# Deformable sampling: ScalarE forms distances and hats of four steps at a time, in place of two

## The chip, the cores and the metric

The kernel runs on one core of one Trainium2 chip. The metric is the device time of one execution in microseconds. Three runs of the kernel before stand for it; their median is 12080.69 us.

## What is computed

The reference is a chain of four layers on x of 2x192x96x96 (f32), each of which normalises x in groups, applies its block and adds the result to x. The change concerns the first, a pair of deformable 3x3 convolutions on 180 channels:

```python
xr = conv1x1(x, w_reduce, b_reduce)
offs = conv1x1(xr, w_offset, b_offset)
off_w, off_h = (offs[:, :cm], offs[:, cm:])
f_w = deform_conv2d(xr, off_w, w_dcnw, b_dcnw)
f_h = deform_conv2d(xr, off_h, w_dcnh, b_dcnh)
f_avg = (f_w + f_h).mean(axis=(2, 3), keepdims=True)
attn = jax.nn.softmax(conv1x1(f_avg, w_attn, b_attn), axis=1)
f_dcm = attn[:, 0:1] * f_h + attn[:, 1:2] * f_w
return conv1x1(f_dcm, w_expand, b_expand)
```

Each output pixel reads, for each of 10 channel groups and 9 taps, xr at a place given by an offset, interpolated between four pixels. The other layers (an edge filter with a 1x1 convolution, a recurrent mixing in two directions, a selective scan) aren't touched.

## The kernel before

`program` runs nine phases one after another; only `sample_and_convolve` is changed. It treats the image as 144 tiles of 128 pixels (72 in each of two images), 12 tiles to a turn of the loop. A tile has 20 steps: two convolutions times ten channel groups. Two neighbouring steps are a pair and share one slot of the buffer HX, which has RP = 8 slots. A tile reads five, five or six candidate rows in turn (`ROWSOF`); the number sets how wide the sampling matmuls are (90 or 108 columns).

Sampling along x is a matmul with interpolation weights, max(0, 1-|x-p|), as the matrix. Five engines work on it, each with an order of its own, written out by hand and held together by semaphores:

- SyncE, `pair_load` (L790 to L794): waits for a free slot (s_free, L791), then loads the sampling places of one pair, broadcast to 96 partitions, 2304 elements in each (864 KB), and raises the slot's own semaphore s_bx. Eight slots are free at the start. Every third tile the input rows are loaded too (`chunk_load`, L766, 675 KB), behind the first pair of that tile; row data, sums and stores of a tile are issued between pairs.
- ScalarE, `distance` (L828 to L831): waits for the slot's s_bx and writes |place - p| in place; `hats` (L833 to L837): waits for one distance to be done (s_ab, L835) and writes max(0, 1-d) in place, and raises s_hx by 2, one for each step. `row_weights` (L839 to L850) does four small instructions in each tile for the weights along y (Abs at L847, Relu at L850; the waits for VectorE are L843 and L845). Its loop runs AHEAD = 12 steps ahead by index: at step n it issues the distance of pair (n+12)/2+1 and then the hats of pair (n+12)/2. The small ones come at steps 4, 5, 9 and 10 of a tile.
- TensorE: at step n (two at a time) it transposes what VectorE summed (L912), then calls `sample` for steps n+6 and n+7. Each first waits for s_pt (L918) and then for s_hx (L879), and makes 18 matmuls (36 records) at L884. Then it convolves (L925). The first of these matmuls gives back one slot (s_free).
- VectorE multiplies the samples with the weights along y (`weigh`, L1019) and, with GpSimd (`halve`, L955), sums over rows; s_pt comes out of this.

```python
                    for n in range(NBB):
                        i, j = n // NB, n % NB
                        if n % 2 == 0:
                            distance((n + AHEAD) // 2 + 1)
                            hats((n + AHEAD) // 2)
                        if j in (4, 5, 9, 10):
                            row_weights((i + 1) % NRB, (4, 5, 9, 10).index(j))
```

Of the kernel before, what the change touches and what calls it, by code (L numbers as in the profile page):

```python
# [9 lines left out]
ACT = mybir.ActivationFunctionType  # L10
# [687 lines left out]
def sample_and_convolve(nc, k):  # L698
# [10 lines left out]
    NRB = 12  # L709
    NBB = NB * NRB  # L710
    NPX = TAPS * 128
    RP, AHEAD, LEAD = 8, 12, 6
    EXTRA = AHEAD // 2 + 1
    LEN = TAPS * CG
    NPR = NG // 2
    pieces = [range(2 * LEN * g // 128, 2 * LEN * (g + 1) // 128) for g in range(NPR - 1)]
# [1 line left out]
    with Phase(nc, "dc") as p:  # L718
# [4 lines left out]
        HX = p.sb([W, RP, 2, NPX])  # L723
# [9 lines left out]
        QX = p.sb([W, 1])  # L733
# [8 lines left out]
        s_bx = p.sems(RP)  # L742
# [6 lines left out]
        def loops(e, body):  # L749
            nw = e.value_load(k.FLAG[0:1, 0:1], min_val=1, max_val=NWIN)  # L750
            for b in range(B):
                for y2 in range(NT // NRB):
                    with e.Fori(0, nw) as w:
                        body(b, y2, w)

        with p.block() as blk:
            @blk.sync
            def _(e):
# [10 lines left out]
                def row_loads(i, b, ti, y):  # L769
                    for h in range(2):  # L770
                        at = 384 * (y // 3) + 64 * TILES[y % 3][h]
                        e.dma_start(OYT[64 * h:64 * h + 64, i % 2, :], k.oyd_v[b][at:at + 64]).then_inc(s_row[i % 2], 16)
                    e.dma_start(TAB[:, i % 2, :],
                                k.d["c_tab"][DS(ti, 1)].rearrange("a p c -> (a p) c")).then_inc(s_row[i % 2], 16)
# [5 lines left out]
                def store_tile(i, at, sem):  # L780

                    e.wait_ge(s_out, 2).then_inc(s_out, -2)
                    dst = k.d["fd"][DS(at, 1)].rearrange("y c (h p) x -> p (c h) (y x)", p=HM)
                    e.dma_start(dst, FT[:, i % 2, :, :]).then_inc(sem, 16)
# [5 lines left out]
                def pair_load(slot, b, y, q):  # L790
                    e.wait_ge(s_free, 1).then_inc(s_free, -1)  # L791
                    src = k.d["sxd"][b, DS(y, 1)].rearrange("a c (q k) x -> (a c q) (k x)", q=5)
                    src = src[q:q + 1, :].partition_broadcast(W)
                    e.dma_start(HX[:, slot, :, :].rearrange("p u n -> p (u n)"), src).then_inc(s_bx[slot], 16)  # L794
# [17 lines left out]
                row_loads(0, 0, 0, 0)  # L812
                for q in range(EXTRA):
                    pair_load(q, 0, 0, q)
                    if q == 0:
                        chunk_load(0, 0, 0)
                e.wait_ge(s_sb, 16).then_inc(s_sb, -16)
                e.wait_ge(s_free, RP + 2 - EXTRA).then_inc(s_free, EXTRA - 2 - RP)
                store_tile(0, B * NT, s_fin)
# [3 lines left out]
            @blk.scalar  # L823
            def _(e):
                e.dma_start(WD[:, :, :, :], k.d["w_dcn"]).then_inc(s_w, 16)
                e.wait_ge(s_qx, 16).then_inc(s_qx, -16)

                def distance(q):  # L828

                    e.wait_ge(s_bx[q % RP], 16).then_inc(s_bx[q % RP], -16)  # L830
                    e.activation(HX[:, q % RP, :, :], HX[:, q % RP, :, :], ACT.Abs, bias=QX[:, 0:1]).then_inc(s_ab, 1)  # L831

                def hats(q):  # L833

                    e.wait_ge(s_ab, 1).then_inc(s_ab, -1)  # L835
                    e.activation(HX[:, q % RP, :, :], HX[:, q % RP, :, :], ACT.Relu, bias=1.0, scale=-1.0)\  # L836
                        .then_inc(s_hx, 2)  # L837

                def row_weights(i, step):  # L839

                    o = slice(step // 2 * HM * ROWSOF[i % 3], (step // 2 + 1) * HM * ROWSOF[i % 3])
                    if step % 2 == 0:
                        e.wait_ge(s_rw, 2).then_inc(s_rw, -2)  # L843
                    if step == 0:
                        e.wait_ge(s_hyf, 1).then_inc(s_hyf, -1)  # L845
                    if step % 2 == 0:
                        e.activation(V[:, o], V[:, o], ACT.Abs).then_inc(s_va2, 1)  # L847
                    else:
                        e.wait_ge(s_va2, 1).then_inc(s_va2, -1)
                        e.activation(HY[:, i % 2, o], V[:, o], ACT.Relu, bias=1.0, scale=-1.0).then_inc(s_hy, 1)  # L850

                for step in range(4):
                    row_weights(0, step)
                distance(0)
                for q in range(AHEAD // 2):
                    distance(q + 1)
                    hats(q)

                def body(b, y2, w):
                    for n in range(NBB):  # L860
                        i, j = n // NB, n % NB
                        if n % 2 == 0:
                            distance((n + AHEAD) // 2 + 1)
                            hats((n + AHEAD) // 2)
                        if j in (4, 5, 9, 10):
                            row_weights((i + 1) % NRB, (4, 5, 9, 10).index(j))

                loops(e, body)
                e.wait_ge(s_ab, 1).then_inc(s_ab, -1)
                e.wait_ge(s_hyf, 1).then_inc(s_hyf, -1)  # L870
# [1440 lines left out]
def mamba_scan(nc, k):  # L2311
# [8 lines left out]
    with Phase(nc, "ms") as p:  # L2320
# [256 lines left out]
        with p.block() as blk:  # L2577
# [12 lines left out]


PHASES = (first_norm_and_projections, far_samples, sample_and_convolve, mix_and_expand, edges_and_merge,
          wkv, gate_and_project, mamba_inputs, mamba_scan)

# [121 lines left out]
```

## Time and profile before

| | |
|---|---|
| median of three runs | 12080.69 us (12080.34 to 12087.21) |
| the profiled execution's own time | 12053.83 us |
| its span | 12051.9 us |
| mean granted clock of TensorE | 0.955 |
| busy: TensorE / ScalarE / VectorE / GpSimd | 11074.3 / 10353.3 / 9815.6 / 5059.6 us |
| the sampling stage | about 620 to 7220 us |

Busy time is the union of an engine's instructions. Matmuls are pipelined and their ends are modelled, so a matmul row's length holds a small overlap with the next row; starts are the better measure. "Idle before" is the time an engine stood still ahead of an instruction, with what ended it. A name such as "PEq L879" is a semaphore wait of that line on the engine's own queue. Where several waits stand at one place, the trace names one of them, and it may have been another that held.

### The profile page before, as it was taken

The numbers are of one execution on the slowest core, as the hardware profiler recorded it, in microseconds if no ns is written. First come the engines' busy times: TensorE is split into PE (matmuls) and PEld (weight loads), VectorE is DVE, ScalarE is ACT, GpSimd is POOL, SyncE is SP. The second block draws the span as 40 slices with busy tenths as digits, with TensorE's granted clock in tenths as the row PEclk, the third lists the DMA queues.
The fourth block names the chain that finished last, engine by engine and source line by source line (L and its number), as shares of the span: only waits on it lengthen the run. The fifth ranks groups of instructions, "written<-read, shape, count | busy, mean of one in ns | idle before, by whom it ended". The sixth has DMA issues, their size and how long they took to land. (4 is left out here: it accounts for less than half of the span.)

```text
span 12051.9 us, 337397 instructions
## 1 busy us (share of the span) xinstructions
PE 11074.3 (92%) x133078; PEld 8457.9 (70%) x133078; DVE 9815.6 (81%) x14111; ACT 10353.3 (86%) x10426; POOL 5059.6 (42%) x3633
## 2 busy tenths in 40 slices
PE   6689999999999999999999999850899899999999
PEld 4389999999999999999999984420633455555555
DVE  4578888888888888888888886799878788888888
ACT  3299999999999999999999993596778899998998
POOL 0033333333333433343333430133200588888887
PEclk9899999999999999999999995985999899999999
DMA  6488888888888888888888888444544333333332
GB/s 165 129 223 213 214 218 217 218 214 211 215 214 214 217 216 219 218 219 216 215 216 215 219 205 198 136 163 132 171 150 156 116 101 102 108 101 103 101 101 85
DMA packets 818421, 2128.02 MB, mean 177 GB/s; under 512 B 145699, under 2 KB 414369, under 8 KB 674497
## 3 DMA queue, kind: packets, MB, share of 16 engines
q1 hardware_dynamic: 800912, 2072.13, 64.3%
q10 hardware_dynamic: 15120, 30.71, 0.7%
q8 instruction: 1080, 17.69, 0.7%
q14 instruction: 477, 3.90, 0.1%
q0 software_dynamic: 832, 3.59, 0.1%
HBM read 1782.85 MB, written 323.30 MB: 175 GB/s over the span
## 5 line engine op out<-in xcount | busy, mean ns | idle before, releaser
L884 PE MATMUL dc_p<-dc_t 96*64 96x90 f32 (+1 forms) x103896 | 4658.9, 247 | 144.9 <-issue 71.7
L884 PEld LDWEIGHTS dc_p<-dc_t 96*64 96x64 f32 x103896 | 4370.8, 136 | 418.1 <-issue 416.4
L955 POOL TENSOR_TENSOR dc_t<-dc_t 128x324 f32<-128x324 f32 (+1 forms) x2885 | 2591.8, 898 | 4028.3 <-DVEq L1043 2738.2
L1019 DVE TENSOR_TENSOR dc_t<-dc_p,dc_t 128x810 f32<-128x810 f32 (+1 forms) x2886 | 3043.5, 1055 | 896.4 <-DVEq L1016 861.1
L831 ACT ACTIVATE dc_t<-dc_t 96x2304 f32<-96x2304 f32 x1447 | 3189.0, 2204 | 105.6 <-ACTq L830 104.5
L836 ACT ACTIVATE dc_t<-dc_t 96x2304 f32<-96x2304 f32 x1446 | 3049.9, 2109 | 0.0
L2545 DVE TENSOR_TENSOR_SCAN ms_t<-ms_t,ms_p 128x512 f32<-128x512 f32 x1728 | 2127.0, 1270 | 283.7 <-PE ms_p L2487 203.7
L2461 POOL TENSOR_TENSOR ms_t<-ms_t 128x1536 f32<-128x1536 f32 x576 | 1987.9, 3456 | 503.3 <-DVE ms_t L2545 499.6
L2497 PE MATMUL ms_p<-ms_t,top_t 128*128 128x512 f32 x3456 | 1774.7, 596 | 0.0
L925 PE MATMUL dc_p<-dc_t 128*128 128x180 f32 (+1 forms) x7488 | 1536.5, 337 | 3.4 <-issue 2.0
L2487 PEld LDWEIGHTS ms_p<-top_t,ms_t 128*128 128x128 f32 x6912 | 850.9, 141 | 966.4 <-issue 693.8
L925 PEld LDWEIGHTS dc_p<-dc_t 128*128 128x128 f32 (+1 forms) x7488 | 1137.7, 190 | 177.7 <-issue 9.2
L2433 ACT ACTIVATE ms_t<-ms_t 128x384 f32<-128x384 f32 x2304 | 1222.2, 602 | 24.2 <-PE ms_p L2487 24.1
L2440 ACT ACTIVATE ms_t<-ms_t 128x512 f32<-128x512 f32 x1728 | 1114.1, 708 | 0.0
L2487 PE MATMUL ms_p<-top_t,ms_t 128*128 128x128 f32 x6912 | 1049.3, 275 | 56.4 <-DVE ms_t L2545 50.5
L1045 DVE TENSOR_TENSOR dc_t<-dc_t 128x324 f32<-128x324 f32 x1442 | 730.8, 507 | 0.0
L1005 DVE COPY dc_t<-dc_p 128x256 f32<-128x256 f32 (+1 forms) x1440 | 673.8, 468 | 11.7 <-DVEq L1000 7.5
L912 PE MATMUL dc_p<-top_t,dc_t 128*128 128x128 f32 (+1 forms) x3744 | 646.9, 273 | 0.6 <-issue 0.3
L979 DVE TENSOR_TENSOR dc_t<-dc_t 128x225 f32<-128x225 f32 (+1 forms) x580 | 410.2, 708 | 250.6 <-DVEq L977 250.4
L2497 PEld LDWEIGHTS ms_p<-ms_t,top_t 128*128 128x128 f32 x3456 | 522.2, 191 | 15.7 <-DVE ms_t L2555 11.4
L912 PEld LDWEIGHTS dc_p<-top_t,dc_t 128*128 128x128 f32 (+1 forms) x3744 | 496.2, 140 | 18.9 <-issue 1.4
L1034 DVE TENSOR_TENSOR dc_t<-dc_t 128x324 f32<-128x324 f32 x962 | 465.2, 484 | 0.4 <-issue 0.2
(258 smaller groups left out, 9527.7 us busy)
## 6 DMA issues: line engine op xcount, KB each, us to landing
dc_t<-sxd SPq DMA_DIRECT2D x1447, 864.0 KB, 6.1
ms_t<-bcd SPq DMA_DIRECT2D x576, 256.0 KB, 3.3
dc_t<-xrT SPq DMA_DIRECT2D x49, 675.0 KB, 9.7
kvd<-wk_t SPq DMA_DIRECT2D x18, 1536.0 KB, 5.1
szd<-mi_t SPq DMA_DIRECT2D x36, 768.0 KB, 4.4
xvd<-mi_t SPq DMA_DIRECT2D x36, 768.0 KB, 4.8
dld<-mi_t SPq DMA_DIRECT2D x36, 768.0 KB, 3.4
ms_t<-dld SPq DMA_DIRECT2D x36, 768.0 KB, 6.8
```

The lines of the kernel that those rows point to most:

```text
L831: e.activation(HX[:, q % RP, :, :], HX[:, q % RP, :, :], ACT.Abs, bias=QX[:, 0:1]).then_inc(s_ab, 1)
L836: e.activation(HX[:, q % RP, :, :], HX[:, q % RP, :, :], ACT.Relu, bias=1.0, scale=-1.0)\
L884: ins = e.matmul(PT[j % 2][o:o + 64, t // 3, t % 3 * nr * CG:(t % 3 + 1) * nr * CG], HX[:, m // 2 % RP, m % 2, t * 128 + o:t * 128 + o + 6 ...
L912: ins = e.transpose(PR[0:o, u * 128:(u + 1) * 128], VA[:, n // NG % 2, 128 * c:128 * c + o], k.ident[:, :])
L925: ins = e.matmul(PF[:, conv * CM:(conv + 1) * CM], VT[0:o, n // 2 % 2, u, :], WD[0:o, c, conv, :], start=(c == 0), stop=(c == NCK - 1), sk ...
L955: e.tensor_tensor(ZH[:, n % 4, :, 0:m], z[:, :, 0:m], z[:, :, nr * CG - m:nr * CG], ALU.add)\
L1019: e.tensor_tensor(Zt[:, n % 4, 0:nr * LEN].rearrange("p (b m i) -> p b m i", b=3, i=CG), PT[n % 2][:, :, 0:3 * nr * CG].rearrange("p b (m ...
L2433: ins = e.activation(BU[:, i % RT, tb, :], UT[:, c % 2, tb, 0:DI], ACT.Copy, scale=UT[:, c % 2, tb, DI + n:DI + n + 1])
L2461: e.tensor_tensor(G[:, i % RG, :, :], HH[:, i % RH, :, :], CB[:, i % RB, :].unsqueeze(1).to_broadcast([128, ND, T]), ALU.mult).then_inc(s_ ...
L2487: ins = e.transpose(PB[:, d, tb * 128:(tb + 1) * 128], BU[:, i % RT, tb, d * 128:(d + 1) * 128], k.ident[:, :])
L2497: e.matmul(PY[:, d, :], k.ident[:, :], G[:, i % RG, d, :], start=(n == 0), stop=(n == NS - 1))\
L2545: e.tensor_tensor_scan(HH[:, i % RH, d, :], DA[:, i % RA, d, :], PB[:, d, :], CAR[:, n, d:d + 1], ALU.mult, ALU.add).then_inc(s_scan, 1)
```

## The change

ScalarE treats two slots, four steps, in one instruction. `distance` waits for the loads of both slots and `hats` raises s_hx by 4. The loop goes over every fourth step: at step n it issues the distance of quad (n+12)/4+1 and the hats of quad (n+12)/4. The small instructions of a tile come at its steps 4 and 8: the first of two between distance and hats, the second behind the hats. EXTRA, the number of loads issued behind the loop so that ScalarE's lead is served, is 8 in place of 7. The number of slots, the loads, TensorE's order and where it gives slots back, VectorE and GpSimd are as before.

```diff
-    EXTRA = AHEAD // 2 + 1
+    EXTRA = AHEAD // 2 + 2
...
-                def distance(q):
-
-                    e.wait_ge(s_bx[q % RP], 16).then_inc(s_bx[q % RP], -16)
-                    e.activation(HX[:, q % RP, :, :], HX[:, q % RP, :, :], ACT.Abs, bias=QX[:, 0:1]).then_inc(s_ab, 1)
-
-                def hats(q):
-
+                def distance(r):
+
+                    o = 2 * r % RP
+                    e.wait_ge(s_bx[o], 16).then_inc(s_bx[o], -16)
+                    e.wait_ge(s_bx[o + 1], 16).then_inc(s_bx[o + 1], -16)
+                    e.activation(HX[:, o:o + 2, :, :], HX[:, o:o + 2, :, :], ACT.Abs, bias=QX[:, 0:1]).then_inc(s_ab, 1)
+
+                def hats(r):
+
+                    o = 2 * r % RP
                     e.wait_ge(s_ab, 1).then_inc(s_ab, -1)
-                    e.activation(HX[:, q % RP, :, :], HX[:, q % RP, :, :], ACT.Relu, bias=1.0, scale=-1.0)\
-                        .then_inc(s_hx, 2)
+                    e.activation(HX[:, o:o + 2, :, :], HX[:, o:o + 2, :, :], ACT.Relu, bias=1.0, scale=-1.0)\
+                        .then_inc(s_hx, 4)
...
-                for q in range(AHEAD // 2):
-                    distance(q + 1)
-                    hats(q)
+                for r in range(AHEAD // 4):
+                    distance(r + 1)
+                    hats(r)
...
-                    for n in range(NBB):
+                    for n in range(0, NBB, 4):
                         i, j = n // NB, n % NB
-                        if n % 2 == 0:
-                            distance((n + AHEAD) // 2 + 1)
-                            hats((n + AHEAD) // 2)
-                        if j in (4, 5, 9, 10):
-                            row_weights((i + 1) % NRB, (4, 5, 9, 10).index(j))
+                        distance((n + AHEAD) // 4 + 1)
+                        if j in (4, 8):
+                            row_weights((i + 1) % NRB, j // 2 - 2)
+                        hats((n + AHEAD) // 4)
+                        if j in (4, 8):
+                            row_weights((i + 1) % NRB, j // 2 - 1)
```

Lines below move down by up to 5: distance is L833, hats L839, row weights L850 and L853 in the changed kernel.

ScalarE's order at the start of the loop, first before and then changed. dc_s49 to dc_s56 are s_bx of the eight slots (a slot's load has landed), dc_s22 is s_ab (a distance is done), dc_s34, dc_s35 and dc_s37 are the row weights' own; L831 and L833 are distances, L836 and L839 hats, the 128x450 rows are row weights:

```order
L831 ACTIVATE dc_t<-dc_t 96x2304 [waits dc_s56]
L836 ACTIVATE dc_t<-dc_t 96x2304 [waits dc_s22]
L831 ACTIVATE dc_t<-dc_t 96x2304 [waits dc_s49]
L836 ACTIVATE dc_t<-dc_t 96x2304 [waits dc_s22]
L831 ACTIVATE dc_t<-dc_t 96x2304 [waits dc_s50]
L836 ACTIVATE dc_t<-dc_t 96x2304 [waits dc_s22]
L847 ACTIVATE dc_t<-dc_t 128x450 [waits dc_s34,dc_s35]
L850 ACTIVATE dc_t<-dc_t 128x450 [waits dc_s37]
```

```order
L833 ACTIVATE dc_t<-dc_t 96x4608 [waits dc_s49,dc_s50]
L839 ACTIVATE dc_t<-dc_t 96x4608 [waits dc_s22]
L833 ACTIVATE dc_t<-dc_t 96x4608 [waits dc_s51,dc_s52]
L850 ACTIVATE dc_t<-dc_t 128x450 [waits dc_s34,dc_s35]
L839 ACTIVATE dc_t<-dc_t 96x4608 [waits dc_s22]
L853 ACTIVATE dc_t<-dc_t 128x450 [waits dc_s37]
L833 ACTIVATE dc_t<-dc_t 96x4608 [waits dc_s53,dc_s54]
L850 ACTIVATE dc_t<-dc_t 128x450 [waits dc_s34]
L839 ACTIVATE dc_t<-dc_t 96x4608 [waits dc_s22]
L853 ACTIVATE dc_t<-dc_t 128x450 [waits dc_s37]
```

Before, each distance waits for one load, and the hats behind it are those of the slot before. Now each distance waits for two, so the hats of four steps have two more loads ahead of them, and two small instructions stand one on each side of the hats.

ScalarE's order ahead of the loop, where the first hats are made, before and then changed:

```order
L831 ACTIVATE dc_t<-dc_t 96x2304 [waits dc_s49]
L831 ACTIVATE dc_t<-dc_t 96x2304 [waits dc_s50]
L836 ACTIVATE dc_t<-dc_t 96x2304 [waits dc_s22]
L831 ACTIVATE dc_t<-dc_t 96x2304 [waits dc_s51]
L836 ACTIVATE dc_t<-dc_t 96x2304 [waits dc_s22]
```

```order
L833 ACTIVATE dc_t<-dc_t 96x4608 [waits dc_s49,dc_s50]
L833 ACTIVATE dc_t<-dc_t 96x4608 [waits dc_s51,dc_s52]
L839 ACTIVATE dc_t<-dc_t 96x4608 [waits dc_s22]
L833 ACTIVATE dc_t<-dc_t 96x4608 [waits dc_s53,dc_s54]
L839 ACTIVATE dc_t<-dc_t 96x4608 [waits dc_s22]
```

The first hats stood behind two loads and two distances of 2304 elements; now they stand behind four loads and two distances of 4608.

## Rows read from the trace of the kernel before

**Rows 1.** Windows: length; busy PE, PEld, DVE, ACT, POOL; granted clock, DMA share, GB/s.

```profile
620.00:7220.00 6600.00, 6474.70 (x115705) 6009.12 (x115706) 5427.51 (x9082) 6293.03 (x3469) 2591.75 (x2885) 0.99 0.85 216
...
4053.00:4058.00 5.00, 4.60 (x42) 4.32 (x42) 2.72 (x4) 4.84 (x3) 1.06 (x2) 0.66 0.40 92
```

**Rows 2.** Costliest groups: xcount | busy us, mean ns | idle before, releaser.

```profile
L831 ACT ACTIVATE dc_t<-dc_t 96x2304 f32<-96x2304 f32 x1447 | 3189.0, 2204 | 105.6 <-ACTq L830 104.5
L836 ACT ACTIVATE dc_t<-dc_t 96x2304 f32<-96x2304 f32 x1446 | 3049.9, 2109 | 0.0
```

**Rows 3.** Waits, 700 to 7300 us: waiter <- ended by: us, times, longest.

```profile
ACT dc_t L847 <- ACTq L845: 177.2, 126, 3.3
...
PE dc_p L884 <- issue: 68.1, 81, 2.5
...
PE dc_p L884 <- PEq L879: 31.6, 49, 2.8
```

**Rows 4.** Waits of SyncE's queue, 3000 to 5000 us.

```profile
SPq L791 <- SPq L791: 1645.2, 439, 8.9
```

**Rows 5.** Timeline of TensorE: start us, length us, line, count.

```profile
4021.03 3.55 PE L884 MATMUL dc_p<-dc_t 96*64 96x108 f32 x72
...
4045.03 3.55 PE L884 MATMUL dc_p<-dc_t 96*64 96x108 f32 x72
...
4053.40 2.61 PE L884 MATMUL dc_p<-dc_t 96*64 96x108 f32 x34 [1.70 <-issue]
...
4072.68 3.01 PE L884 MATMUL dc_p<-dc_t 96*64 96x90 f32 x72
...
4081.14 3.01 PE L884 MATMUL dc_p<-dc_t 96*64 96x90 f32 x72
4084.08 1.18 PE L925 MATMUL dc_p<-dc_t 128*128 128x180 f32 x6
...
4093.98 3.01 PE L884 MATMUL dc_p<-dc_t 96*64 96x90 f32 x72
...
4098.06 3.01 PE L884 MATMUL dc_p<-dc_t 96*64 96x90 f32 x72
...
4138.34 3.01 PE L884 MATMUL dc_p<-dc_t 96*64 96x90 f32 x72 [0.94 <-PEq L879]
...
4197.99 3.55 PE L884 MATMUL dc_p<-dc_t 96*64 96x108 f32 x72
```

**Rows 6.** Pair loads L794: one near 4084.7, one near 4182.8, then all 439 of 3000 to 5000.

```profile
L794 SPq DMA_DIRECT2D dc_t<-sxd x1: 303/303/303, 4084.7 to 4084.7; - x1
...
DMA to landing us min/median/max: 6.1/6.1/6.1
...
L794 SPq DMA_DIRECT2D dc_t<-sxd x1: 310/310/310, 4182.8 to 4182.8; - x1
...
DMA to landing us min/median/max: 8.9/8.9/8.9
...
DMA to landing us min/median/max: 5.2/6.1/10.5
```

**Rows 7.** Timeline of ScalarE.

```profile
4084.30 2.11 ACT L836 ACTIVATE dc_t<-dc_t 96x2304 f32<-96x2304 f32 x1
4086.31 2.20 ACT L831 ACTIVATE dc_t<-dc_t 96x2304 f32<-96x2304 f32 x1
4088.42 2.11 ACT L836 ACTIVATE dc_t<-dc_t 96x2304 f32<-96x2304 f32 x1
4090.97 2.22 ACT L831 ACTIVATE dc_t<-dc_t 96x2304 f32<-96x2304 f32 x1 [0.45 <-ACTq L830]
...
4125.51 2.11 ACT L836 ACTIVATE dc_t<-dc_t 96x2304 f32<-96x2304 f32 x1
```

**Rows 8.** ScalarE's groups by shape, 800 to 7100 us.

```profile
L850 ACT ACTIVATE dc_t<-dc_t 128x450 f32<-128x450 f32 x185 | 105.8, 572 | 10.9
...
L850 ACT ACTIVATE dc_t<-dc_t 128x540 f32<-128x540 f32 x92 | 59.5, 647 | 5.4
```

## The prediction

> **What bounds the kernel now.** First I read the windows of the trace to find the stage: the change lies wholly between 620 and 7220 us. There the matmul rows of TensorE cover 6474.7 of 6600 us, ScalarE's 6293.0, VectorE's 5427.5, and the DMA engines are busy 0.85 of the time [rows 1]. TensorE sets the pace; all that could ever be won on it here is the 125 us in which it is idle. Then the groups: distance and hats (2204 and 2109 ns each, 2304 elements) make up almost all of ScalarE's time, and before the distances it stood idle for loads for 104.5 us in all [rows 2]. Third, the waits: TensorE's own at the sampling line are few (68.1 and 31.6 us), and ScalarE's longest is the one ahead of the row weights (177.2 us, L845) [rows 3]. The 31.6 us carry the name L879, which is the wait for hats. But one of them ends at 4138.34 [rows 5], and the hats of that pair were written by 4125.51+2.11 = 4127.62 [rows 7]: they had been ready for 10.7 us, so another wait of the same place held TensorE, the one for VectorE's and GpSimd's work on the sums (s_pt). SyncE waits before every load it issues [rows 4]: L791 is the wait for a free slot (439 waits for 439 loads), so a load starts as soon as TensorE gives one back. So three engines run round a ring: slot freed, load, distance, hats, sampling, slot freed. What matters is how much slack this ring has, not how busy ScalarE is.
>
> I number the pairs of steps (a slot holds one pair) 0, 1, 2, ... through the stage. When the pair p has been sampled, TensorE's next matmul at L925 frees the slot for load p+7. An example: sampling ends and L925 starts at 4084.08 [rows 5]; the load is issued at 4084.7 and lands 6.1 us later [rows 6]; the distance of that pair starts at 4090.97, at once [rows 7]. The pair two before it in the slots has its hats at 4084.30 to 4086.41 [rows 7] and wasn't sampled until 4098.06 [rows 5]: pair 756, ready 11.7 us early. That float of 10 to 12 us is why TensorE doesn't wait for ScalarE today.
>
> **The change, part by part.** *ScalarE's own work.* Now a distance is followed by its neighbour 2.11 us later and hats by theirs 2.01 us later (4086.31, 4088.42 and the rows around) [rows 7]. The element rate comes from the row weights: 90 elements more take 647-572 = 75 ns, 0.83 ns each [rows 8], so 2304 more elements add 1.92 us. For four steps: 4.03+3.93 = 7.96 us instead of 2x4.12 = 8.24. That is 0.28 us saved in each of 720 quads, 202 us of ScalarE's time. None of it is on the path, since TensorE doesn't wait for ScalarE: the cover is the float, which the next part spends.
>
> *What the quad waits for.* Before, the hats of pair p needed load p+1 (the distance of p+1 is issued ahead of them). Now the hats of pairs p, p+1 (p even) need load p+3, because the distance ahead of them covers p+2 and p+3. Nothing is loaded earlier: there are still eight slots, freed one by one at the same matmul, and SyncE issues the same loads in the same order, save one more at the end. So the wait ends two pairs later, 8.5 to 9.6 us, and both instructions behind it run 1.92 us longer before anything of them counts, together 12.4 to 13.4 us later. Against the float the ring closes or falls short.
>
> *The ring, counted directly.* From the issue of load p+3 to the start of sampling pair p TensorE walks four pairs less one sampling, and less the 0.66 us between L925 and the issue. In a tile with five candidate rows five pairs take 4093.98-4072.68 = 21.30 us, 4.26 each, and a sampling 2.94 (its 3.01 less the overlap); in one with six rows 4045.03-4021.03 = 24.00, 4.80 each, and 3.48 [rows 5]. So there are 4x4.26-0.66-2.94 = 13.4 us, or 4x4.80-0.66-3.48 = 15.1 us. The chain wants landing 6.1 (the median of 439 [rows 6]), 0.11 to the distance, 4.03 for it and 4.03 for the hats: 14.3 us.
> - Five rows: short by 0.8 us. In the example: hats would end at 4090.97+8.06 = 4099.03, sampling was due at 4098.06, short by 0.97.
> - Six rows: 0.8 us to spare.
> - In two quads of five (loop index j 4 and 8) a row-weights instruction now stands between distance and hats. It takes 572 or 647 ns [rows 8], and less the overlap of some 0.1 us that neighbours on ScalarE show (hats 2.11 long, the next start 2.01 later [rows 7]) I take 0.5.
> - Every third tile SyncE loads the 675 KB of input rows behind the tile's first pair, and the next pair, an odd one, which is the kind a quad waits for, lands late: 8.9 us in the example. From 4182.8 to 4197.99, when pair 778 was sampled, are 15.2 us [rows 6, 5]; wanted are 8.9+0.11+8.06+0.5 = 17.6: short by 2.4.
>
> *The sum.* Three tiles hold 15 quads. Ten of them have five rows: 10x0.83 + 4x0.5 = 10.3 us short. But the window of each quad also holds TensorE's wait at the quad before, so a steady shortness is paid once in two quads: 5.2 us. Plus 2.4 for the late load: 7.6 us per three tiles, 48 times in 144 tiles, 365 us. From this I take off two things. A wait before an even pair leaves a gap ahead of the odd load, which then lands sooner; landings range down to 5.2 us [rows 6], and I take 0.2 us of relief, near the median since the DMA engines stay busy: 10x0.2/2x48 = 48. And some of the new waits fall where TensorE is idle anyway; of the 125 us [rows 1] I take a quarter, 30. I add 12 us once at the start, where the first hats now need four loads rather than two (864 KB at 216 GB/s, 4.1 us each [rows 1]) and both instructions are 1.92 us longer. VectorE and GpSimd do the same as before and wait as they do now; their slack grows, cost 0. The waits of ScalarE ahead of the row weights [rows 3] will mostly go, since the weights now come after a later load; nothing is gained by it. Net: 365-48-30+12 = +299 us. Against the profiled execution's 12053.8 that is 12353; the median of the runs shown, 12080.7, is 27 us above it, so I forecast 12380.
>
> The ends. Were every critical load to land at 5.2, the shortness of five-row quads goes and the late load costs 1.5: 48x1.5+12 = 84 us, 12165. Were no wait shared between quads, 48x(10.3+2.4) = 610 us, 12690; since the window argument excludes most of that, I go a good half of the way.
>
> **The rivals.**
> *A. The clock falls at the new waits.* After a wait of 1.70 us (the row at 4053.40) 34 matmuls took 2.61 us, where 72 take 3.55 otherwise, and the granted clock of the 5 us window there is 0.66 [rows 5, 1]. Part of those 5 us ran at the lower level, 1.2 GHz; 5x(1-0.66) = 1.7 us of work were lost. For it: the waits behind the late loads are 2.4 us. Against: the common ones are under 1 us, and the wait of 0.94 us before 4138.34 was followed by a normal 3.01 [rows 5]. At 48 such places: 82 us more, 12460. Chance 0.2.
> *B. Faster: the saved overhead counts.* In five-row tiles ScalarE's ten pairs (41.2) and four weights (about 2) fill more than TensorE's 42.6 us. If TensorE's present waits come from ScalarE's lateness, the 202 us remove them. This decides if landings shrink below about 5.3 us, so that the ring closes in all tiles. Price: the half of 125 us, 12020. Against: hats stood ready 10.7 and 11.7 us ahead, in one case at the very wait that carries the hats' line as its name. Chance 0.07. The Trainium skill, Advanced Engine Details and Errata, section TRN2 Errata, holds that a bubble stands between ScalarE instructions and advises large tiles to make it small: by that rule this change is a gain. The rows agree that it saves ScalarE 0.28 us a quad; they don't show that this time is on the path.
> *C. No difference: the ring gives way.* With TensorE slower, traffic falls: in the 5 us window after that stall the DMA share was 0.40 [rows 1]. If landings drop near 5.2 and late ones hide in existing waits, only the start's 12 us are left: 12093. Against: the late load is slow because 1539 KB are in flight, and a short wait doesn't change that. Chance 0.08. The Trainium skill, DMA: Bandwidth & Descriptors, section Latency and other measured facts, has the fixed part of a transfer shrink when HBM is less loaded, which speaks for C; the spread of landings agrees in direction, and no row here gives the size at an idle HBM.
>
> **How the numbers follow.** Forecast 0.65, A 0.20, B 0.07, C 0.08. A measurement of this kernel can tell about 0.2%, 24 us, from no change. So slower 0.85, same 0.08, faster 0.07. The range takes in the forecast's own low end, A, and half of the way to the high end: 12165 to 12560; it leaves out B and C.
>
> **What would show it.** In the changed profile: distance and hats near 4120 and 4030 ns, 720-odd each; the stage about 300 us longer, with TensorE waiting at the sampling line in the first sampling of a quad, 0.5 to 1 us in five-row tiles, longest (2 to 3 us) once in three tiles; ScalarE waiting for loads at the distance (hundreds of us, not 104), and hardly ahead of the row weights; DMA share under 0.85. Wrong if TensorE's idle time in the stage stays at 125 us (C) or falls (B); if granted clock falls well under 0.99, A.

## The result and the profile after

The changed kernel takes 12520.52 us in the median of four runs (12499.26 to 12524.19), the kernel before on the same chip 12083.95 us. The ratio is 1.0354, with a 95% interval of 1.0336 to 1.0372: slower by 3.5%, 437 us. The forecast was 12380 in a range of 12165 to 12560, so the sign and the range hold, and the loss forecast, 299 us, is two thirds of the one measured.

The page of the changed kernel, busy time by engine and the groups that answer to [rows 2] (xcount | busy, mean ns | idle before, releaser):

```profile
span 12497.3 us, 335231 instructions
...
PE 11186.5 (90%) x133078; PEld 8553.3 (68%) x133078; DVE 9834.1 (79%) x14111; ACT 10170.4 (81%) x8980; POOL 5009.1 (40%) x3633
...
L888 PE MATMUL dc_p<-dc_t 96*64 96x90 f32 (+1 forms) x103896 | 4740.3, 250 | 481.1 <-PEq L883 379.5
...
L833 ACT ACTIVATE dc_t<-dc_t 96x4608 f32<-96x4608 f32 x724 | 2994.6, 4136 | 937.8 <-ACTq L832 935.9
L839 ACT ACTIVATE dc_t<-dc_t 96x4608 f32<-96x4608 f32 x723 | 2913.6, 4030 | 0.0
```

ScalarE did what was intended: 183 us less busy time (10170.4; 10353.3 before). It now stands idle for 936 us ahead of the distances, waiting for loads (104.5 before). TensorE's idle time ahead of the sampling matmuls went from 144.9 us (the page before, L884) to 481.1, and its busy time for the same 133078 matmuls from 11074.3 to 11186.5. These two, 336 and 112 us, come to 448 us; the span grew by 445. Taken from the trace, the stage from its first sampling to its last takes 7019 us, 6586 before: 433 of the 445 us lie in it.

The waits from 700 to 7700 us, as in [rows 3]; L883 is the wait for hats, L832 the wait for the quad's second load:

```profile
ACT dc_t L833 <- ACTq L832: 918.7, 543, 7.1
...
PE dc_p L888 <- PEq L883: 333.4, 314, 5.2
...
PE dc_p L888 <- issue: 95.8, 91, 2.7
```

The 49 waits under the hats' line have become 314, and now the name is right: 315 quads behind the first find TensorE waiting at their start, and in 312 of them sampling starts within 0.2 us of the hats' end. The ring, followed once round at pair 736: the last load that its hats need, that of pair 739, is issued at 4193.0 and lands 6.0 us later; then ScalarE, then TensorE's sampling:

```profile
L794 SPq DMA_DIRECT2D dc_t<-sxd x1: 303/303/303, 4193.0 to 4193.0; - x1
...
DMA to landing us min/median/max: 6.0/6.0/6.0
```

```profile
4199.13 4.14 ACT L833 ACTIVATE dc_t<-dc_t 96x4608 f32<-96x4608 f32 x1 [6.18 <-ACTq L832]
4203.18 4.03 ACT L839 ACTIVATE dc_t<-dc_t 96x4608 f32<-96x4608 f32 x1
```

The sampling row is cut off by the end of the window that was asked for:

```profile
4207.35 0.88 PE L888 MATMUL dc_p<-dc_t 96*64 96x90 f32 x17 [0.96 <-PEq L883]
```

The distance starts 0.1 us behind the landing, the hats 4.05 us later, they end at 4207.21, and sampling starts 0.14 us after. Nothing in this chain waits for anything but its forerunner. TensorE waited 0.96 us for it, in the place and of the size that the forecast named for a five-row tile.

And the late load behind the input rows. TensorE waits 2.33 us for it in the mean of its 48 times. The longest of these waits, behind a load that landed 11.7 us after its issue (9.65 in the mean of the 48), in the timeline of TensorE, with the windows around it (length; busy PE, PEld, DVE, ACT, POOL; granted clock, DMA share, GB/s):

```profile
4107.40 3.55 PE L888 MATMUL dc_p<-dc_t 96*64 96x108 f32 x72
...
4117.52 6.63 PE L888 MATMUL dc_p<-dc_t 96*64 96x108 f32 x72 [5.24 <-PEq L883]
```

```profile
620.00:7640.00 7020.00, 6572.71 (x115539) 6093.57 (x115540) 5437.03 (x9067) 6091.94 (x2019) 2538.07 (x2880) 0.98 0.79 202
...
4117.00:4124.00 7.00, 6.48 (x72) 6.44 (x72) 1.57 (x2) 7.00 (x5) 1.06 (x1) 0.51 0.06 18
```

After a wait of 5.24 us the 72 matmuls of a six-row pair took 6.63 us instead of 3.55; the granted clock of that window is 0.51, the lower level, 1.2 GHz. That is 3.1 us on top of the wait. Counted over the whole stage, 55 pairs have sampling matmuls that take over 0.33 us each (0.24 to 0.26 otherwise), 18 before; 31 of the 55 stand right behind the wait for the late load.

### The profile page after: what moved, and what is told of

It is laid out like the page before. It is cut to its first block and busy times, and to the rows that moved or that the text cites. A ratio compares the mean times of both kernels' runs of the same rounds, so it can differ in the third digit from the quotient of the medians.

```text
span 12497.3 us, 335231 instructions
## 1 busy us (share of the span) xinstructions
PE 11186.5 (90%) x133078; PEld 8553.3 (68%) x133078; DVE 9834.1 (79%) x14111; ACT 10170.4 (81%) x8980; POOL 5009.1 (40%) x3633
## 5 line engine op out<-in xcount | busy, mean ns | idle before, releaser
L888 PE MATMUL dc_p<-dc_t 96*64 96x90 f32 (+1 forms) x103896 | 4740.3, 250 | 481.1 <-PEq L883 379.5
L888 PEld LDWEIGHTS dc_p<-dc_t 96*64 96x64 f32 x103896 | 4455.7, 138 | 770.1 <-issue 767.3
L959 POOL TENSOR_TENSOR dc_t<-dc_t 128x324 f32<-128x324 f32 (+1 forms) x2885 | 2541.9, 881 | 4518.6 <-DVEq L1047 2920.9
L833 ACT ACTIVATE dc_t<-dc_t 96x4608 f32<-96x4608 f32 x724 | 2994.6, 4136 | 937.8 <-ACTq L832 935.9
L839 ACT ACTIVATE dc_t<-dc_t 96x4608 f32<-96x4608 f32 x723 | 2913.6, 4030 | 0.0
```

What stands on the lines that cost most here:

```text
L833: e.activation(HX[:, o:o + 2, :, :], HX[:, o:o + 2, :, :], ACT.Abs, bias=QX[:, 0:1]).then_inc(s_ab, 1)
L839: e.activation(HX[:, o:o + 2, :, :], HX[:, o:o + 2, :, :], ACT.Relu, bias=1.0, scale=-1.0)\
L888: ins = e.matmul(PT[j % 2][o:o + 64, t // 3, t % 3 * nr * CG:(t % 3 + 1) * nr * CG], HX[:, m // 2 % RP, m % 2, t * 128 + o:t * 128 + o + 6 ...
L959: e.tensor_tensor(ZH[:, n % 4, :, 0:m], z[:, :, 0:m], z[:, :, nr * CG - m:nr * CG], ALU.add)\
```

## The experiments

The theory: the loss is the ring's lateness, counted from the landing of load p+3 to the sampling of pair p, plus the clock that falls after the longest waits. The rivals: the long instructions cost by themselves; waiting for two loads at once costs, whatever comes behind; ScalarE's order doesn't matter; the kernel before was held by ScalarE's fullness. Each kernel ran in turn with the kernel before on the same chip; ratios are to that. Two experiments are compared by their ratios too, since the kernel before has medians from 12067 to 12084 us in the three sets of runs.

**e1: short instructions, long waits.** The changed kernel's order and waits, with instructions of one slot:

```diff
-                    e.activation(HX[:, o:o + 2, :, :], HX[:, o:o + 2, :, :], ACT.Abs, bias=QX[:, 0:1]).then_inc(s_ab, 1)
+                    for u in range(2):
+                        e.activation(HX[:, o + u, :, :], HX[:, o + u, :, :], ACT.Abs, bias=QX[:, 0:1]).then_inc(s_ab, 1)
...
+                    for u in range(2):
+                        e.wait_ge(s_ab, 1).then_inc(s_ab, -1)
+                        e.activation(HX[:, o + u, :, :], HX[:, o + u, :, :], ACT.Relu, bias=1.0, scale=-1.0)\
+                            .then_inc(s_hx, 2)
```

> Instructions of 2304 elements again, but in the changed kernel's order and with its waits (two loads, distance, distance, hats, hats). Ring theory (loss = how late the first hats of a quad end against TensorE's four-pair window): the first hats end 2.11+2.11+2.11 = 6.3 us after the loads instead of 8.06, 1.75 us sooner. Five-row quads then have about 0.8 us to spare, only the late load behind the input rows is still short, by 1 us at most: 12130 to 12200 us, TensorE idle in the stage about 170 us. Rival (waiting for two loads at once costs, whatever the instructions' length): stays near 12520. Rival (the long instructions themselves cost): back to 12084.

Measured: 12175.78 us, ratio 1.0077 (1.0059 to 1.0094). The two loads are waited for just as in the changed kernel, but four fifths of the loss are gone. Handing over the first half of a quad 1.75 us sooner is enough for most quads. So waiting for two loads at once is not what costs, whatever comes behind. The first rival, that the long instructions cost by themselves, asked for the whole loss to go, and 0.8% stays; this run alone doesn't settle it, e2 does. TensorE's idle time ahead of sampling shows the remnant:

```profile
L890 PE MATMUL dc_p<-dc_t 96*64 96x90 f32 (+1 forms) x103896 | 4675.8, 247 | 242.1 <-PEq L885 125.6
```

**e2: long instructions, short wait.** Hats directly behind their own distance, so that they need load p+1:

```diff
-                        distance((n + AHEAD) // 4 + 1)
+                        distance((n + AHEAD) // 4)
```

(and the same ahead of the loop, with 6 loads behind it instead of 8).

> Instructions of 4608 elements, but the hats of a quad come directly behind its own distance, so they need load p+1 and no longer load p+3. Ring theory: the window is six pairs, 22 us, against 6.1+0.1+8.1+0.5 = 14.8 us, 7 us to spare: TensorE's waits are back at about 100 us, time 12060 to 12110. Rival (the hats wait for the distance to drain, 0.1 to 0.3 us in each quad, and ScalarE, at 42.4 of 44.4 us per tile, becomes the bound in five-row tiles): 12120 to 12250. Rival (long instructions cost by themselves): near 12520.

Measured: 12056.46 us, ratio 0.9990 (0.9980 to 0.9999), just under the range expected and no difference that counts. The 4608-element instructions are all there, and the loss is all gone; they cost nothing by themselves. The order's own price can be read on ScalarE: hats that need the distance just ahead start 4.24 us behind it (4023.28 to 4027.52) and not 4.05, 0.2 us in each quad, hidden.

```profile
4023.28 4.12 ACT L833 ACTIVATE dc_t<-dc_t 96x4608 f32<-96x4608 f32 x1
4027.52 4.05 ACT L839 ACTIVATE dc_t<-dc_t 96x4608 f32<-96x4608 f32 x1
```

**e3: the input rows' load one pair later in the queue.** In the changed kernel:

```diff
-                            if q == 0 and i % 3 == 0:
+                            if q == 1 and i % 3 == 0:
```

> The changed kernel with the 675 KB load of input rows issued behind the second pair of the tile (an even pair is late then) rather than the first. Ring theory: the waits of 5 us once in three tiles, 2.6 us above the kernel before, shrink to those of the next odd pair, landing near 7.6: -70 us; and most of the half-clock stretches (29 of 51 stand at this quad), 1.7 us each, go: -50. Time 12350 to 12430. Rival (the late load is a small part, the loss is spread over all quads): 12480 to 12520.

Measured: 12334.89 us, ratio 1.0210 (1.0193 to 1.0227); 186 us less than the changed kernel by the medians, 174 by the ratios, more than expected. One `if` on a load that occurs 48 times is worth two fifths of the loss, 3.6 to 3.9 us each time.

```profile
PE 11126.8 (90%) x133078; PEld 8488.2 (69%) x133078; DVE 9830.7 (80%) x14111; ACT 10170.9 (82%) x8980; POOL 5015.3 (41%) x3633
...
L888 PE MATMUL dc_p<-dc_t 96*64 96x90 f32 (+1 forms) x103896 | 4684.4, 248 | 377.3 <-PEq L883 275.0
```

Between the two profiled executions idle time fell by 104 us and busy time by 60: over a third of what this load had cost was the clock behind its waits and not the waits. The pairs with slow matmuls are down from 55 to 24.

**e4: no row weights between distance and hats.** In the changed kernel both small instructions stand behind the hats:

```diff
-                        if j in (4, 8):
-                            row_weights((i + 1) % NRB, j // 2 - 2)
                         hats((n + AHEAD) // 4)
+                        if j in (4, 8):
+                            row_weights((i + 1) % NRB, j // 2 - 2)
```

> The changed kernel with both row-weights instructions of a place behind the hats, none between distance and hats. Ring theory: 0.5 us less in two quads of five, shared between neighbours, 144x2x0.25 to 144x2x0.5 = 70 to 140 us less, minus what the next distance is late by: 12380 to 12470. Rival (ScalarE's order doesn't matter, only its lateness in all): 12500 to 12530.

Measured: 12422.12 us, ratio 1.0294 (1.0277 to 1.0311): 98 us less than the changed kernel by the medians, 72 by the ratios, for half a microsecond moved 288 times, 0.25 to 0.34 us each. ScalarE has the same instructions as before the edit; only their order changed. TensorE's idle time ahead of sampling is 72 us less, its busy time (11157.7 us) 29 us less:

```profile
L888 PE MATMUL dc_p<-dc_t 96*64 96x90 f32 (+1 forms) x103896 | 4736.5, 249 | 409.5 <-PEq L883 307.9
```

**e5 and e6: ten slots.** `RP` is 10 instead of 8 (the buffer still fits), in the changed kernel (e5) and in the kernel before (e6):

```diff
-    RP, AHEAD, LEAD = 8, 12, 6
+    RP, AHEAD, LEAD = 10, 12, 6
```

> The changed kernel with ten slots in HX instead of eight. Ring theory: the window grows by two pairs, 8.5 us and more, so no quad is short: TensorE's waits are back at about 100 us, time 12050 to 12110. Rival (long instructions, or ScalarE's coarser handing over, cost by themselves): 12200 or more.

> The kernel before (pairs in each instruction) with ten slots instead of eight. If the 1.4% that ten slots gained over the kernel before come from loads that SyncE issues two pairs earlier (the row data among them, for which VectorE waits 230 us today), this is as fast as the changed kernel with ten slots: 11890 to 11940. Rival (the gain needs the 0.28 us a quad that long instructions save ScalarE, which with pairs is fuller than TensorE in five-row tiles): 11960 to 12040.

Measured: e5 11911.32 us, ratio 0.9862 (0.9846 to 0.9879); e6 11913.08 us, ratio 0.9869 (0.9853 to 0.9886). With ten slots the changed kernel doesn't lose, as the ring asks. I had expected no better than the kernel before, and both are 1.3% faster than it. And they are equal, by their ratios as well as by their medians: with room in the ring, the 198 us that ScalarE is busy for less (10136.1 against 10334.5) are worth nothing.

The sampling rows of e5, then of e6, show TensorE's idle time under the 144.9 us of before:

```profile
L888 PE MATMUL dc_p<-dc_t 96*64 96x90 f32 (+1 forms) x103896 | 4618.5, 247 | 59.5 <-PEq L883 45.3
```

```profile
L884 PE MATMUL dc_p<-dc_t 96*64 96x90 f32 (+1 forms) x103896 | 4621.7, 247 | 50.3 <-PEq L879 37.3
```

**e7 and e8: row data one pair earlier.** Where did the extra 150 us come from? Another wait of the kernel before that wasn't in my account is VectorE's at its row sums (waits, 700 to 7300 us):

```profile
DVE dc_t L979 <- DVEq L977: 232.2, 142, 4.6
```

L977 waits for a tile's row data, three small loads that stand in SyncE's order behind the last pair load of the tile before. SyncE issues them only when a slot has come free. Ten slots bring that two pairs forward, and between 700 and 7700 us neither e5 nor e6 has a wait left there; one edit of the order brings it one pair forward:

```diff
-                        row_loads(i, b, ti, y)
+                        if i == 0:
+                            row_loads(i, b, ti, y)
...
+                            if q == 9 and i + 1 < NRB:
+                                row_loads(i + 1, b, e.snap(t0 + w + (y + 1) * NWIN), y + 1)
```

e7 is this edit in the kernel before, e8 the same in e2.

> The kernel before, eight slots, with the small loads of a tile's row data issued one pair earlier in SyncE's order (11 of 12 tiles). Theory (TensorE's present 100 us of waits and 30 us of lower clock come from VectorE waiting for row data that SyncE can't issue while it waits for a slot): VectorE's 230 us at the row sums fall under 40, time 11940 to 12000. Rival (those waits come from ScalarE's fullness or from chance): 12050 to 12084, no change.

> Four steps in each instruction, hats behind their own distance, eight slots, and row data issued one pair earlier: both theories together. Float 7 us as in the run without the early row data, TensorE's waits gone: 11900 to 11980, faster than the kernel before by over 1%. Rival (ScalarE's waits for row sums were not what held TensorE): 12040 to 12060.

Measured: e7 11936.98 us, ratio 0.9892 (0.9875 to 0.9909); e8 11928.19 us, ratio 0.9878 (0.9861 to 0.9894). Both are as expected or 3 us better. (The rival of e8 speaks of ScalarE's waits for row sums; VectorE's are meant.) In e7 VectorE's wait of 232 us is down to 9 and TensorE's waits at the sampling line from 68.1 and 31.6 us to 20:

```profile
PE dc_p L887 <- issue: 20.0, 35, 1.5
DVE dc_t L982 <- DVEq L980: 8.8, 12, 1.5
```

So the last rival falls too: what held TensorE in the kernel before was VectorE without its row data, and ScalarE is as full in e7 as it was.

## Why the prediction came out as it did

The forecast of 12380 was 140 us short of the result. The mechanism held; the result lies in the range because the range was drawn far enough to take in rival A.

- *TensorE sets the pace and ScalarE's saved time is off the path.* Right. ScalarE's busy time fell by 183 us (forecast 202) and that bought nothing, in the changed kernel or with ten slots (e5 against e6, 2 us apart).
- *Distance and hats near 4120 and 4030 ns.* Right: 4136 and 4030.
- *The hats of a quad need load p+3, and the ring is short by about 0.8 us in five-row tiles.* Right in mechanism: e1 and e2 undo it by either of its two ends, e5 by the slots. The chain is 0.14 us longer than I counted, the step from the hats' end to the start of sampling, which I had left out. The ten short quads in three tiles are not quite the ones named: the window begins four pairs ahead of the sampling, so the first quad of a six-row tile, whose window lies in the five-row tile before it, waits 0.77 us in the mean of 48, and the first quad of the next five-row tile never.
- *TensorE's added idle time.* The sum of 299 us was all for this; measured 336. Term by term, from TensorE's waits at the start of each quad in the trace: the late quads 112 us (the sum had 115), the others 215 (248 less 48 of relief, 200), the very first 7.4 more (44.1 after 36.6; the sum had 12). The term that failed is the 30 us taken off for waits that would fall where TensorE is idle anyway: its other waits at the sampling line came to 108 us before and to 110 now, so nothing was hidden in them. That is most of the 37 us that the sum fell short in idle time.
- *The relief and the row weights.* The relief of 0.2 us in landings was about right: their median fell from 6.1 [rows 6] to 5.9 us. For the row weights I had charged half a microsecond in four of ten five-row quads, shared, and in the late quad, 72 us in all; e4 took as much off TensorE's idle time.
- *The late load costs 2.4 us once in three tiles.* Right. Taken from the trace over the 48 quads that wait for it, TensorE waits 2.33 us in the mean, 112 us in all, where it didn't wait once before the change; the load lands 9.65 us after its issue in the mean, 9.55 before. That e3 gained 174 to 186 us by moving it, and not 112, is the next point.
- *The clock.* The forecast left it at nothing and gave it to rival A, 82 us at a chance of 0.2. It happened: 112 us more busy time on the same matmuls, 108 of it in this stage, with 55 pairs of slow matmuls in place of 18. This is the step that failed, the one that set the clock's price in the sum to nothing. The row was there [rows 5, 1]: a wait of 1.70 us had brought the clock down, and the sum held waits of 2.4 us 48 times. Nor is it every such wait: of the 77 pairs that held a wait of over 1.5 us, 48 ran slow matmuls (10 of 19 before). Forecast and rival A weren't alternatives; the second follows from the first, and their sum, 12460, is within half a percent of the result.
- *Rival B (faster).* It named the right pool, TensorE's own waits, and the wrong key. The pool could be won (e6, e7), not by ScalarE.
- *Rival C (the ring gives way).* It didn't: the DMA share fell from 0.85 to 0.79 and the median landing by 0.2 us, far too little to close a gap of 0.8 us. The Trainium skill, DMA: Bandwidth & Descriptors, section Latency and other measured facts, has the fixed part of a transfer shrink when HBM is less loaded. The direction of these landings agrees.
- *ScalarE's waits ahead of the row weights will mostly go.* Right: 177 us before, no such row after.

## What to carry to other kernels

Before two steps are merged into one instruction, count what the first consumer must now wait for: here one fixed cost of 0.28 us per quad was saved and 12 to 13 us of lead were spent, on a ring that had 11.7. A merged instruction needs a merged buffer: more slots, or an order without look-ahead (e2), make the merge free; they don't make it pay while another engine sets the pace. And if waits are forecast that are as long as one after which the trace shows a lower clock, add the clock to the same sum, with a share of the waits and not all of them (48 of 77 here).

## What the runs showed that I had not expected

- Once in three tiles one transfer of 675 KB, issued one place too early in a queue, cost 3.6 to 3.9 us each time (e3), two fifths of the whole loss, over a third of it as clock.
- The kernel before had 1.1 to 1.3% to give, in SyncE's order: three small loads stuck behind a wait for a slot they don't need. VectorE's wait for them is 232 us, TensorE's waits 100 us. Ten slots (11911 us) or the loads one pair earlier (11937 us) bring it in; the gain, 138 to 161 us by the medians, is more than TensorE's waits, since its busy time falls as well, from 11074.3 to 11019.3 us in e7:

```profile
PE 11019.3 (92%) x133078; PEld 8426.1 (71%) x133078; DVE 9888.0 (83%) x14111; ACT 10346.3 (87%) x10426; POOL 4979.5 (42%) x3633
```

- Hats that depend on the instruction directly ahead start 0.2 us later than independent ones (4.24 against 4.05 us behind a 4608-element distance).
